# Pairwise projections, unringed queries, clearing on ScalarE, reordered attention steps and a third weighted-value buffer in a four-layer graph network

## The reference, cut to what matters

```python
x = _layernorm(x + L0(x, ...))   # sums of neighbours, 16 relations over 2 bases
x = _layernorm(x + L1(x, ...))   # two sub-layers, 32 relations over 4 bases, tanh
x = _layernorm(x + L2(x, ...))   # relu((sum of neighbours) @ W.T + b)
x = _layernorm(x + L3(x, ...))   # attention over the edges:
#   q = (x@Wq+bq)*scale; k = x@Wk+bk; v = x@Wv+bv       (8 heads of 16)
#   s = sum_d q[dst]*k[src]; softmax of s over the edges of each dst
#   out = segment_sum(attn * v[src], dst)
```

## Time and profile before

| | us |
|---|---|
| median of 3 runs (2339.98 to 2342.94) | 2340.57 |
| the profiled execution's own time | 2338.07 |
| its span, first to last instruction | 2336.1 |
| sums stages end, projections begin | 1641 |
| attention gathers begin | 1715.3 |
| queries stored, clearing begins | 1742 to 1744 |
| last attention gather ends | 2271.75 |

### The profile page before, as it was taken

The page is one execution under the profiler, slowest core; times in us unless marked ns, Lnnn a source line. Parts: engine busy times, 40 slices in busy tenths (PEclk is TensorE's granted clock), DMA queues, the critical chain, the costliest instruction groups (busy, mean ns, idle before and its releaser), DMA issues.

```text
span 2336.1 us, 32097 instructions
## 1 busy us (share of the span) xinstructions
PE 1630.6 (70%) x8440; PEld 1237.9 (53%) x8464; DVE 1551.0 (66%) x5276; ACT 418.9 (18%) x891; POOL 1636.3 (70%) x1687
## 2 busy tenths in 40 slices
PE   4877777775767676765567667667536888888886
PEld 3555555553555554544444444444425777767775
DVE  8776776775666666664355555556767877787785
ACT  0000000002000000002111111111124444443442
POOL 7777777775777777775777777774247777777760
PEclk9555555555555656675587777687555555555555
DMA  5233233232233233235232332332444333333330
GB/s 139 56 84 85 57 84 84 56 85 71 57 84 85 84 84 112 57 84 155 54 98 84 98 98 84 98 99 80 62 128 112 109 106 108 107 106 106 108 97 6
DMA packets 149414, 207.36 MB, mean 89 GB/s; under 512 B 48568, under 2 KB 111019, under 8 KB 149120
## 3 DMA queue, kind: packets, MB, share of 16 engines
q0 software_dynamic: 61280, 138.20, 22.1%
q1 hardware_dynamic: 86802, 65.12, 9.3%
q10 hardware_dynamic: 1154, 1.99, 0.3%
HBM read 172.41 MB, written 36.04 MB: 89 GB/s over the span
## 4 chain that ended last, share of the span: by engine, by line
POOL 41%; PE 21%; issue 17%; DVE 9%; DMA 8%; ACT 3%; DVEq 0%; ACTq 0%; POOLq 0%; SPq 0%
POOL G L529 41%; PE p_w L1432 6%; PE p_g L594 4%; DMA G<-h_d,idx 3%; DMA G<-in_x,idx 3%; PE p_oh L1385 2%; PE p_w L1435 2%; DVE hs L1639 1%; PE p_d L640 1%; DVE XH L1633 1%; PE p_o L625 1%; PE p_d L605 1%; ACT oht L1515 1%; DMA q_d<-work 1%; DMA kv_d<-kv_s 1%
## 5 line engine op out<-in xcount | busy, mean ns | idle before, releaser
L529 POOL DMA_INDIRECT G<-h_d,idx x832 | 793.1, 953 | 283.9 <-issue 261.6
L594 PE MATMUL p_g<-S,G 128*128 128x96 f32 (+1 forms) x2496 | 604.5, 388 | 468.1 <-DMA G<-h_d,idx 286.8
L594 PEld LDWEIGHTS p_g<-S,G 128*128 128x128 f32 x2496 | 521.9, 290 | 670.9 <-issue 301.8
L1365 POOL DMA_INDIRECT G<-kv_d,idx x416 | 430.0, 1034 | 186.1 <-issue 185.8
L529 POOL DMA_INDIRECT G<-in_x,idx x416 | 401.1, 964 | 132.6 <-issue 119.2
L944 DVE TENSOR_SCALAR work<-iota_h,key_f 128x600 bf16<-128x600 f16 x416 | 171.9, 413 | 260.7 <-PE p_d L605 260.1
L919 DVE SCALAR_TENSOR_TENSOR S<-con,rel,shared 128x96 f32<-128x96 f32 (+1 forms) x1248 | 315.7, 294 | 0.7
L605 PE MATMUL p_d<-work 128*128 128x312 bf16 (+1 forms) x832 | 268.7, 423 | 23.7 <-DVE work L959 22.7
L937 DVE TENSOR_TENSOR agg<-agg,p_g 128x96 f32 (+1 forms) x624 | 144.5, 232 | 108.6 <-PE p_g L594 86.8
L1432 PE MATMUL p_w<-S,PV 128*128 128x40 f32 x832 | 199.2, 415 | 0.7 <-DVE PV L1700 0.7
L959 DVE TENSOR_TENSOR work<-work,p_d 128x312 f32 (+1 forms) x416 | 191.3, 460 | 10.9 <-issue 10.0
(11 more groups left out here) (246 smaller groups left out, 2077.7 us busy)
## 6 DMA issues: line engine op xcount, KB each, us to landing
work<-A_d SPq DMA_DIRECT2D x25, 800.0 KB, 4.5
A_d<-work SPq DMA_DIRECT2D x12, 1600.0 KB, 7.4
G<-h_d,idx POOLq DMA_INDIRECT x832, 2.5
G<-in_x,idx POOLq DMA_INDIRECT x416, 2.5
G<-kv_d,idx POOLq DMA_INDIRECT x416, 2.8
h_d<-XH SPq DMA_DIRECT2D x75, 64.0 KB
h_d<-in_x SPq DMA_DIRECT2D x2, 1600.0 KB, 7.6
kv_d<-kv_s SPq DMA_DIRECT2D x25, 128.0 KB, 1.7
```

The costliest lines, as they stand in the source:

```text
L529: pool.indirect_dma_start(G[:, c % GRING, :], None, l.table, bass.IndirectOffsetOnAxis(ap=l.places[:, c:c + 1], axis=0)).then_inc(s_arr[g ...
L594: last = pe.matmul(p_g[:, g % PB, 0:width], G[:, c % GRING, :], S[:, c % (SRING * GR), 0:width], start=(k == 0), stop=(k == GR - 1))
L1365: pool.indirect_dma_start(G[:, c % KRING, :], None, d["kv"], bass.IndirectOffsetOnAxis(ap=idx[:, c:c + 1], axis=0)).then_inc(s_arr[c // QC ...
```

## The change

- **Projections by pairs.** All of `post_body` up to the keys and values runs over `DUOS` = 13 pairs of tiles. One DVE instruction does what two did, except for the statistics and the normalising, which stay one for each tile but stand back to back. `kv_s` holds three pairs; a pair is stored by one DMA of 256 KB.
- **Order in the projections.** DVE takes the keys and values of pair u-2 between the front and the back of pair u. The chunk tables stand in pairs 3 to 9, two in each, where they stood one in each tile from the 11th on; their second half (negate and scale) goes to ACT. `dT` lies in another buffer.
- **Queries without a ring.** `q_p` holds all 25 tiles; `part` waits for no store. SP stores tile by tile with 25 DMAs.
- **Clearing on ScalarE.** `agg` and `SC` of the attention are cleared by ACT in 13 slices each (`wipe`), one slice of each in each pair of the projections. DVE clears only `RB`.
- **Attention steps.** On DVE `products(4k)` stands before `chunk_max`, and `one_hots` works two batches ahead instead of one (it has a step more at the start). On PE two window sums stand no longer together. On ACT the first two `thrice` stand at the beginning of the step, all four before the first `one_hot_copy`. `PV` has three buffers (`VRING`).

```diff
         def last_front(u):
...
+            dve.tensor_tensor(y[:, two, :], p_g[:, u % 3, 0:n * D].rearrange("p (t d) -> p t d", d=D), bc(b_lin, 1, n),
+                              ALU.add).then_inc(s_y0, 1)
+            dve.wait_ge(s_y0, u + 1)
+            dve.scalar_tensor_tensor(y[:, two, :], y[:, two, :], 0.0, XA[:, tiles, :], ALU.max, ALU.add).then_inc(s_y, 1)
+            dve.wait_ge(s_y, u + 1)
+            for j in range(n):
+                last = dve.bn_stats(bn6[:, two.start + j, :], y[:, two.start + j, :])
...
+        def wipe(k):
+            for ap in wiped:
+                n = ap.shape[1]
+                act.activation(ap[:, k * n // DUOS:(k + 1) * n // DUOS],
+                               bc(con[:, C_ONE:C_ONE + 1], 2, (k + 1) * n // DUOS - k * n // DUOS)[:, 0], ACT.Copy,
+                               scale=0.0).then_inc(s_wipe, 1)
+        def chunk_tables(n):
+            two = pen[:, 2 * n:2 * n + 2]
+            act.wait_ge(s_tab, n + 1)
+            act.activation(two, two, ACT.Copy, scale=-LOW, bias=LOW).then_inc(s_pen, 1)
         def part(g, k):
-            if k == 0 and g >= 3:
-                act.wait_ge(s_qst[g % 3], 16 * (g // 3))
...
         def chunk_tables(n):
             if n == 0:
                 dve.wait_ge(s_dT, 16 * CB)
             dve.tensor_tensor(pen[:, two], dT[:, two, 0:P + 1], dT[:, two, 1:P + 2], ALU.is_equal).then_inc(s_tab, 1)
-            dve.wait_ge(s_tab, 8 + 2 * n)
-            dve.tensor_scalar(pen[:, two], pen[:, two], -1.0, -LOW, ALU.add, ALU.mult).then_inc(s_tab, 1)
...
+            for u in range(DUOS + 2):
+                if u < DUOS:
+                    last_front(u)
+                if 0 <= u - 2:
+                    keys_values(u - 2)
+                if u < DUOS:
+                    last_back(u, aside)
+                if 1 <= u < 8:
+                    row_tables(u - 1)
+                if 3 <= u <= 8:
+                    chunk_tables(2 * u - 6)
+                    chunk_tables(2 * u - 5)
...
+            for t in range(NT):
+                sp.wait_ge(s_q[5], t // QG + 1)
+                sp.dma_start(d["q"][t * P:(t + 1) * P, :], q_p[:, t].rearrange("p s d -> p (s d)")).then_inc(s_qst, 16)
...
-    PV = sb("PV", [P, 2, QC, D])
+    PV = sb("PV", [P, VRING, QC, D])
...
         dve.tensor_copy(idb[:], ident)
-        dve.memset(agg[:], 0.0).then_inc(s_pp, 1)
         dve.memset(RB[:], LOW).then_inc(s_pp, 1)
-        dve.memset(SC[:], 0.0).then_inc(s_pp, 1)
...
-            if q >= 2:
-                dve.wait_ge(s_mm, q - 1)
+            if q >= VRING:
+                dve.wait_ge(s_mm, q - VRING + 1)
```

More of the change, by code:

```diff
@@ L206, in _ @@
             def _(act):
-                sums.scalar(act)
+                sums.scalar(act, wiped)
                 att.scalar(act)
@@ L362, in sum_layers @@
     s_kvst = [sem(f"s_kvst{k}") for k in range(3)]
-    s_qst = [sem(f"s_qst{k}") for k in range(QS)]
-    per_pass = range(s_it.num, s_qst[QS - 1].num + 1)
+    s_qst = sem("s_qst")
+    per_pass = range(s_it.num, s_qst.num + 1)
     N_NP, N_LATE, N_SPAN, N_FULL, N_RUNS, N_BAD, N_F, N_NF, N_IT, N_NEG = range(10)
@@ L779, in post_body @@
         def post_body():
-            for i in range(NT + 2):
-                if i < NT:
-                    deviation(i)
-                if 0 <= i - 2 < NT:
-                    last_copy(i - 2)
+            for u in range(DUOS):
+                deviations(u)
+                last_copy(u)
+                wipe(u)
+                if 0 <= u - 5 < KB // 2:
+                    chunk_tables(u - 5)
+            for n in range(DUOS - 5, KB // 2):
+                chunk_tables(n)
             for i in range(QGROUPS + 2):
@@ new lines, in last_back @@
+        def last_back(u, aside):
+            n = min(2, NT - 2 * u)
+            two = slice(u % 2 * 2, u % 2 * 2 + n)
+            dve.wait_ge(s_std, u + 1)
+            dve.reciprocal(rstd[:, two, :], std[:, two, :]).then_inc(s_rs, 1)
+            dve.wait_ge(s_rs, u + 1)
+            for j in range(n):
+                t, k = 2 * u + j, two.start + j
+                last = dve.tensor_scalar(XH[:, t:t + NT + 1, :][:, bass.ds(aside, 1), :].rearrange("p a d -> p (a d)"),
+                                         y[:, k, :], mv[:, k, 0:1], rstd[:, k, :], ALU.subtract, ALU.mult)
+            last.then_inc(s_done, 1)
@@ L1312, in attention @@
     STEPS = range(-1, KB + 3)
+    DVE_STEPS = range(-2, KB + 3)
     def passes(eng, ns, turn, body):
@@ L1466, in body @@
                     queries(4 * k)
+                if old:
+                    window_sums(4 * k - 7)
+                if now:
                     queries(4 * k + 1)
@@ L1563, in body @@
                 mid, nxt = batch(k - 1), batch(k + 1)
+                if nxt:
+                    thrice(4 * k + 4)
+                    thrice(4 * k + 5)
                 if mid:
@@ L1577, in body @@
                 if nxt:
-                    thrice(4 * k + 6)
-                    thrice(4 * k + 7)
                     one_hot_copy(4 * k + 5)
@@ L1771, in vector @@
                     add(4 * k - 8)
+                if now:
+                    products(4 * k, landed)
                 if mid:
@@ L1774, in vector @@
                 if now:
-                    products(4 * k, landed)
                     head_part(4 * k)
@@ L1780, in vector @@
                     row_max(k - 1)
-                if nxt:
-                    one_hots(k + 1)
+                if batch(k + 2):
+                    one_hots(k + 2)
                 if old:
```

220 lines of the change are left out of this document (115 added, 105 removed).

## The result

The changed kernel takes **2319.31 us** (median, 2318.34 to 2319.64), the kernel before 2340.28 beside it: a ratio of 0.9911, 95% interval 0.9893 to 0.9928. It is faster by 0.9%, inside the forecast's own range of 2300 to 2322, and 9 us above its middle: 21 us gained where 30.6 were forecast. The profiled execution's own time is 2318.34, its span 2316.5. The attention's last gather ends at 2273.25, before at 2271.75; the other engines, whose last product came 23 us behind it, now wait for the gathers.

The account below looks back on a forecast made before the run. GpSimd's gathers set the end: starting 10 us earlier, they bring the last product to 2264.5, 30 us earlier, though the engines alone would reach 2237 (26 plus 31 us earlier). Median 2340.57 - 30.6 = 2310 us; own range 2300 to 2322, overall 2289 to 2326.

Parts of the forecast that it names:

- The gathers set the end: Attention: gathers end at 2261.75, so the last product cannot stand before 2264.5, 30 us earlier; 54%.
- Engine steps 1.4 us shorter: Attention steps of the other engines, 21.65 us before: gain between 0 and 3.5, taken as 1.4, over some 22 steps 31 us.
- The waits moved as said: Attention on VectorE: the 2.15 us wait before `values` mostly moves to the addition behind it, which needs the same window sum.
- What a gather takes: GpSimd in the attention: each gather goes on taking 1.34 us, 1.25 bare, with collisions costing 1.6 us a step.
- The slower rival: Attention: VectorE waits for gathers, runs in step with them and locks them out, up to 3.9 us a step; 2375 us; 6%.
- The worst of both at once: Attention: one gather held from the start of `one_hots` to `values`, another through factors and two `values`: 3.9 us a step.
- Projections 10 us earlier: Projections: last keys and values at 1702, so the gathers start 10 us earlier, 7 to 13 with the landing's bounds.
- The stall: Projections: VectorE waits 11 us at the first chunk table, in the fourth pair, until all `dT` loads land near 1667.
- Engines 26 us earlier: Attention start of the engines other than GpSimd: 26 us earlier, 17 from the queries and 9.2 from clearing leaving VectorE.
- The queries had landed: Queries ahead of the attention: last part at about 1721, landed at 1725 instead of 1741.94, 17 us earlier.
- Collide less: Attention rival: collisions cost gathers 0.6 us a step, 26 us less; engines take over at 2237, time about 2284; 13%.
- the row of 2.11 us: Attention, kernel before: gather begun at 2048.15 within `one_hots`, said to speak against descriptor generation not being blocked.

Follow-up runs that it names:

- the program with half of them: Changed kernel with only every second chunk gathered by GpSimd, the others plain SyncE loads in stored order: 2282.37 us, ratio 0.9753.
- the attention's half alone: Kernel before with only the new attention order and three weighted-value buffers; projections, queries and clearing as before: 2319.82 us, ratio 0.9911.
- split order: Changed kernel with `one_hots` moved behind the second products and their sums, third sums between window factors and fade: 2286.33 us, ratio 0.9764.

## Why the prediction came out right, and its mis-sized terms

- **The gathers set the end**: right, shown by the program with half of them (37 us less) and by 66 us of waits for them. Last products stand 2.66 us behind the last gather's end (2275.91 against 2273.25), forecast 2.8; from there to the end of the span 40.6 us, forecast 41.0. The forecast's 30 us were 20 for the engines' lag behind the gathers and 10 for the gathers' earlier start. The lag went, and that is the whole gain, as the attention's half alone shows. The earlier start brought nothing: 6.4 us came, and the gathers gave back 7.9. The time still lies in the range, which allowed 3 us for the projections and 6 or 7 for collisions.
- **Engine steps 1.4 us shorter**: right. 21.65 - 1.4 = 20.25, and 20.20 was measured where nothing but the engines counts. They would have reached the last product at 2237 by the forecast. With half of the gathers it stands at 2241.68, and the first at 1744.55, 3.4 us later than the forecast's 1767.14 - 26. The waits moved as said: `add` and not `values` waits for the window sum.
- **What a gather takes**: the term that was off. The step "if each goes on taking 1.34 us" gave 556.4 us; 564.3 were measured. That is 7.9 of the 11.4 us by which the last product is later than forecast. The slower rival named the mechanism (VectorE waits for gathers, runs in step with them, and the phase is a bad one) but priced it only at its worst, 3.9 us for a step. It happened in a small size. The step shown above, with 2.63 and 1.50 us, loses 2.2 instead of 1.6; over all 26 batches it is 7.9 us, 0.3 for each. The worst of both at once did not occur.
- **Projections 10 us earlier**: 6.4. The stall was 12.8 and not 11, as VectorE went on only at 1669.9, half a microsecond past the late bound of 1669.4 (the last load was issued at 1655.4, and the slowest landed 14.4 us after its issue); the ends wait for TensorE and ScalarE, 1.29 and 0.84 us, which had no term. Last keys and values at 1705.6 and not 1702.
- **Engines 26 us earlier**: 20.75 (first products at 1746.39, before at 1767.14). The queries had landed 11.2 us earlier and not 17 (`idb` at 1731.34, before at 1742.51): ScalarE's last part ended at 1723.53, where about 1721 was forecast, although the keys and values came 3.6 late. The rest is SP: its stores take 0.46 us each (median, one of them 1.18) where 0.4 were assumed, seven of them were still to be issued and not four or five, and from the end of the last, 1727.84, it was 3.5 us to `idb`, where 2.5 were assumed. It cost nothing here.
- **Collide less**, the rival of 2284 at 13%: the changed kernel didn't do it. The split order does, and took 2286.33.
- **What a long gather says**: the prediction set the row of 2.11 us against an inference of the Trainium skill. The row does not contradict it; the last section has the rows that tell the two apart.

The sums stages end 0.5 us later in this trace (1642.86 against 1642.38), which is no part of the change. Sum of the misses at the last product: 0.5 + 3.1 + 7.9 = 11.5 us, less 0.1 in landing; at the end of the span 11.0 (2316.5 against 2305.5). The medians lie 9.3 apart, as the profiled execution is 1 us under its median and the forecast carried the 2.5 of before.

## What to carry to other kernels

When two lines of work run at nearly the same speed, the gain of one ends where the other sets the end; count it only up to there. Then look at what the slower one costs once the faster one waits for it, since the two meet at other places than before. Where GpSimd's gathers set the pace, look at the order of the VectorE instructions with both inputs in SBUF before looking at their number: two runs broken up were worth more than the whole change. And a part that is worth nothing today can be worth 23 us after the next edit, so a measured zero alone is no reason to throw it away.

## What the runs showed of the hardware

A gather takes 0.95 us when nothing holds it. In the changed kernel's trace 41 gathers from 1755 us on take 1.2 us or more. Each of them ends 0.81 to 0.83 us behind a VectorE instruction with both inputs in SBUF (`one_hots`, window factors, `values`), the last of its run. In the trace of the kernel before 43 of 43 do, two of them in the earlier trace rows. An `add` of 0.22 us with one input in PSUM did not let the gather through between two of them (2112.71 above). A gather that has begun well ahead of such a run takes its usual time. In the split order this one, from the program of 2286 us, started 0.20 us ahead of the `one_hots` at 2116.08:

```profile
2115.88 0.95 POOL L1420 DMA_INDIRECT G<-kv_d,idx  x1 [0.30 <-issue]
```

In the changed kernel one that started 0.14 us ahead was held, the longest of all. It ends 0.83 behind the `values` of 2068.07 to 2068.74:

```profile
2066.84 2.73 POOL L1420 DMA_INDIRECT G<-kv_d,idx  x1 [0.30 <-issue]
```

```profile
2066.98 1.01 DVE L1682 TENSOR_TENSOR oh<-con,rel 128x160 bf16<-128x160 f32 x4
```

Both fit a gather that needs what VectorE holds at about 0.13 us after its start (0.95 - 0.82) and never again; that is worked out, not measured. By this estimate a run costs a gather at most its own length. For the 1.76 us of `one_hots` to `values` the row above agrees: 2.73 - 0.95 = 1.78.

Not every gather waits for the end of a run. This one started 0.26 us into the window factors (L1743) and ended 0.34 behind them, though two `values` followed at once. It came in between two of the four:

```profile
2098.50 1.10 POOL L1420 DMA_INDIRECT G<-kv_d,idx  x1 [0.30 <-issue]
```

```profile
2098.24 1.02 DVE L1743 TENSOR_TENSOR S<-con,rel 128x160 f32<-128x160 f32 x4
...
2099.30 1.28 DVE L1756 TENSOR_TENSOR PV<-G,ps 128x512 f32<-128x512 f32 x2
```

What decides whether it gets in is not shown.

The Trainium skill says (SBUF — State Buffer, Who interferes with whom) that such a VectorE instruction and a GpSimd instruction that reads SBUF exclude each other, and infers that generating descriptors is not blocked. These traces agree with both. A gather reads its indices (`idx`) from SBUF and is held. But only its beginning is: the one of 2115.88 took its usual 0.95 us, although `one_hots` ran beside it from 0.20 us after its start on. GpSimd's plain loads of `dT`, which read no indices, were not held. In the kernel before:

```profile
1645.46 10.15 POOL L540 DMA_DIRECT2D G<-in_flat  x16 [1.57 <-issue]
```

```profile
1654.24 0.57 DVE L1112 TENSOR_TENSOR agg<-agg 1x416 f32<-1x416 int32 x1
```

One of the 16 began at 1654.34, 0.10 us into L1112, which has both inputs in SBUF, and took 0.64 us like the median. Held like a gather it would have taken about 0.98 (estimate: to the end of L1112 at 1654.81, and from there 0.64 - 0.13). That it is the reading of the indices is inferred from this difference; no run takes them away.
